# State rows spread by DMA, h in PSUM, sums on PE, and a new order for a batch's chain in a fused Mamba and mixture-of-experts kernel

## Chip, cores and metric

One core of one Trainium2 chip (trn2). The metric is the device time of one execution in microseconds (us).

## What is computed

x is (4, 128, 256): batch, channel, token. Every token is normed over its 128 channels; the channels form 4 chunks of 32 that go through one small Mamba block (inner width 64, 16 states, rank 2):

```python
xz = x @ in_proj.T; xi, z = split(xz)
xc = silu(causal_conv4(xi) + conv_b)
dt, B, C = split(xc @ x_proj.T)
dt = softplus(dt @ dt_proj.T + dt_b)
h = exp(dt * A) * h + (dt * xc) * B[s]        # for each of 16 states s, a scan over tokens
y = (sum_s h * C[s] + xc * D) * silu(z) @ out_proj.T
```

The result plus the scaled input is normed, projected to 128 channels (x1), normed again with the router's norm, and sent through 16 experts of width 256: the two best experts per token get softmax weights, `silu(x Wg) * (x Wu)` is projected back by Wd, weighted and added to x1. All in float32.

## The kernel before

It is written engine by engine with counted semaphores; each engine runs its own list in the order written, SP only issues DMAs. A tile of N = 512 columns holds two chunks of one batch's 256 tokens, its 128 partitions hold 2 x 64 inner channels, so one batch is one tile and the scan has 4 x 16 = 64 steps k (batch k // 16, state k % 16).

One step: ACT writes the decay exp(dt A) into PSUM (`decay`, L434), POOL multiplies dtx = dt xc with the B row of the state (`scan_input`, L286) into u, DVE scans (`scan`, L608) and multiplies h with the C row (`weigh`, L619) into hc. For steps 0 to 31 PE adds hc up in PSUM with an identity matmul (`sum_state`), for steps 32 to 63 POOL adds it to y (`add_state`, L292). B rows go through DRAM: a DMA writes them to B_far and two DMAs per step (L214, each 64 partitions) read one row 64 times into a ring of 4 slots. C rows stay in SBUF, split into two rounded parts (`round_bc`, `bc_rest` L569), and PE spreads them into PSUM with a selection matmul per step (`spread_c`).

The order: a head (loads, norm, projections, convolution, softplus of batch 0), then FIRST = 32 steps with the softplus pieces of batches 1 to 3 at steps 1 to 15 (`factor_1`, `factor_2`, `add_relu`, `scan_source`), then 64 items n = (batch n // 16, expert n % 16), of which the first 32 each have a step (k = 32 + n) beside them. In an item PE does `up` (L853), `down` of two items before (L868), `gate` of the next item (L835), then `spread_c`; ACT does `gate_tanh` (L485) of the next item and a decay; DVE does `gate` (L662), `scan`, `hidden` (L672), then `weigh` of the step before; POOL does u, adds hc, and once per two items multiplies the tokens with a row of gate weights (`scale_tokens`, xs, L316), which an ACT-issued DMA spreads from DRAM (Gs, `spread_gate`).

Between the last step of a batch and its first expert lies a chain of small pieces (`back`): D x and gating (L628, L631), output projection, norm, projection, second norm with the router's logits, top 2, weights, their transposition to rows in DRAM. Two tables, BESIDE_STEPS and BESIDE_ITEMS, say at which of the 16 slots after the batch's last step an engine does which piece; the piece is done at the end of the engine's loop body. `back` on ACT loads the ln and exp table before each reciprocal root and the tanh table after it once the experts run. The first row of gates of the next batch is asked for at item 13 of 16.

The SP list: x, Wg, Wu, rows of batch 0, four steps' B rows, Wd, rows of batch 1, then the rest.

Of the kernel before, what the change touches and what calls it, by code (L numbers as in the profile page):

```python
# [14 lines left out]
P = 128  # L15
# [43 lines left out]
for _name, _width in (("norm_g", 1), ("norm_b", 1), ("proj_b", 1), ("skip", 1), ("conv_w", TAPS), ("conv_b", 1),  # L59
                      ("D", 1), ("dt_b", 1), ("A_log", NS), ("in_x", P), ("in_z", P), ("bc", P), ("dt_in", P),  # L60
                      ("dt_out", P), ("out0", P), ("out1", P), ("proj", P), ("router", E)):
    COLS[_name] = (_at, _at + _width)
    _at += _width
# [3 lines left out]
def build(nc, x, params, gate_w, up_w, down_w, out):  # L67
    with ExitStack() as ctx:
# [20 lines left out]
        def sum_bank(b):  # L89
            return 6 if b < BATCH - 1 else 3  # L90
# [17 lines left out]
        proj_w = sb("proj_w", [P, P])  # L108
        bias = sb("bias", [P, 1])
        shift = sb("shift", [P, 1])  # L110
        iota_e = sb("iota_e", [P, BLK, E])
        unit = sb("unit", [P, 2 * NS])
# [9 lines left out]

        top = sb("top", [P, BLK, 8])
        topi = sb("topi", [P, BLK, 8], U32)
        topf = sb("topf", [P, BLK, 2])
        w01 = sb("w01", [P, BLK, 2])
        e1 = sb("e1", [P, BLK, 1])
        combine = sb("combine", [P, BLK, E])
        CE = sb("CE", [E, BATCH, T])
        Gs = sb("Gs", [P, G_RING, N])  # L130

        xs = sb("xs", [P, 2, N])

# [26 lines left out]
        eps_in, eps, zero, rest_row, quad1, quad2 = (cst[:, i:i + 1] for i in range(6))  # L160
# [771 lines left out]
```

## Time and profile before

| | us |
|---|---|
| median of three runs | 328.30 (328.22 to 331.42) |
| the profiled execution, its own time | 329.45 |
| its span, first to last instruction | 327.6 |
| PE busy, DVE busy, POOL busy, ACT busy | 286.3, 244.3, 179.2, 151.8 |

Times below are from the profiled execution and count from the start of its span. Engines are PE (matmul), DVE (vector), ACT (scalar), POOL (GpSimd), SP (DMA issues). A row of the timeline is start, duration, engine, line, operation, operands; in brackets the idle time before it and the instruction that ended it. Matmuls overlap, and a group's mean mixes instructions in flight: starts, not durations, give PE's rate. Tile names are the profile's: u, h, hc and the B rows are all "ring", th is "dt", hid is "zs" and "y", tn is "xm".

### The profile page before, as it was taken

How to read it: one execution, taken by the hardware profiler on the slowest of the kernel's cores; microseconds unless marked ns; L12 is line 12 of the kernel's file. 1: busy time of each engine (PE TensorE's matmuls, PEld its weight loads, DVE VectorE, ACT ScalarE, POOL GpSimd, SP SyncE). 2: the span in 40 equal slices, each digit the busy share in tenths (PEclk: the TensorE clock that was granted, in tenths of full speed). 3: DMA queues.
4: the chain of work that ended last, by engine and by line, in shares of the span. 5: the costliest groups of instructions: out<-in, count | busy, mean ns of one | idle time of the engine just before them, and what ended most of it. 6: DMA issues, size and time to landing. Idle time of an engine off the chain costs nothing.

```text
span 327.6 us, 3741 instructions
## 1 busy us (share of the span) xinstructions
PE 286.3 (87%) x1120; PEld 199.0 (61%) x1120; DVE 244.3 (75%) x366; ACT 151.8 (46%) x220; POOL 179.2 (55%) x184
## 2 busy tenths in 40 slices
PE   7987397877984798999888899988999999999996
PEld 6734122223431266676566576765688888888885
DVE  2499989999697378898977989797884565555553
ACT  3679546541551334765433365743426363222231
POOL 4001659986357173888799688878861214331310
PEclk9999879996998799999999999999999999999999
DMA  7913975443241330433223423430111111221110
GB/s 261 348 35 107 254 210 168 148 139 127 79 136 57 120 128 33 120 105 96 96 94 125 123 80 114 122 89 19 66 48 44 54 32 34 72 74 58 41 32 18
DMA packets 21621, 33.64 MB, mean 103 GB/s; under 512 B 2848, under 2 KB 8032, under 8 KB 21600
## 3 DMA queue, kind: packets, MB, share of 16 engines
q1 hardware_dynamic: 16720, 24.39, 24.0%
q10 hardware_dynamic: 4880, 9.00, 8.9%
q8 instruction: 9, 0.15, 0.2%
q14 instruction: 12, 0.10, 0.1%
HBM read 32.53 MB, written 0.85 MB: 102 GB/s over the span
## 4 chain that ended last, share of the span: by engine, by line
PE 35%; issue 22%; POOL 15%; DVE 4%; POOLq 0%; DVEq 0%
PE bank L853 10%; PE bank L868 10%; PE bank L835 9%; POOL xs L316 6%; POOL y L292 5%; PE bank L712 4%; POOL ring L286 3%; DVE ring L608 2%; DVE ring L619 2%; POOL chk L304 1%; PE bank L789 0%; PE bank L788 0%; DVE zs L672 0%; POOL w L300 0%; DVE X L676 0%
## 5 line engine op out<-in xcount | busy, mean ns | idle before, releaser
L485 ACT ACTIVATE dt<-bank,cst 128x512 f32<-128x512 f32 x64 | 44.0, 687 | 112.4 <-PE bank L835 112.3
L286 POOL TENSOR_TENSOR ring<-dtx,ring 128x512 f32<-128x512 f32 x64 | 81.0, 1277 | 18.2 <-DVE ring L608 11.4
L608 DVE TENSOR_TENSOR_SCAN ring<-bank,ring 128x512 f32<-128x512 f32 x64 | 77.6, 1213 | 7.1 <-issue 6.7
L853 PE MATMUL bank<-xs,Wu 128*128 128x256 f32 x256 | 68.0, 388 | 10.3 <-POOL xs L316 5.6
L316 POOL TENSOR_TENSOR xs<-xm,Gs 128x512 f32<-128x512 f32 x32 | 41.4, 1294 | 59.1 <-DMA Gs<-CE_far 54.9
L662 DVE SCALAR_TENSOR_TENSOR dt<-dt,bank 128x512 f32<-128x512 f32 x64 | 43.6, 682 | 36.5 <-ACT dt L485 36.5
L835 PE MATMUL bank<-xm,Wg 128*128 128x256 f32 x256 | 65.7, 379 | 0.0
L434 ACT ACTIVATE bank<-dt,cst,A 128x510 f32<-128x510 f32 x64 | 49.7, 777 | 30.4 <-DVE ring L608 28.0
L853 PEld LDWEIGHTS bank<-xs,Wu 128*128 128x128 f32 x256 | 46.3, 190 | 22.6 <-issue 13.0
L835 PEld LDWEIGHTS bank<-xm,Wg 128*128 128x128 f32 x256 | 48.6, 190 | 7.0 <-issue 0.5
L619 DVE TENSOR_TENSOR ring<-ring,bank 128x512 f32<-128x512 f32 x62 | 41.6, 671 | 14.9 <-PE bank L712 14.6
L292 POOL TENSOR_TENSOR y<-y,ring 128x512 f32<-128x512 f32 x30 | 38.2, 1272 | 23.7 <-DVE ring L619 23.5
L712 PE MATMUL bank<-C_rows,sel 64*128 64x512 f32 x64 | 33.7, 528 | 19.2 <-DVE ring L619 13.4
L712 PEld LDWEIGHTS bank<-C_rows,sel 64*128 64x128 f32 x64 | 12.4, 194 | 52.4 <-DVE ring L619 30.8
L712 PE MATMUL bank<-ring,ident 128*128 128x512 f32 x64 | 39.6, 706 | 0.0
L868 PE MATMUL bank<-zs,Wd 128*128 128x256 f32 x128 | 32.9, 380 | 0.2 <-DVE y L628 0.2
L868 PE MATMUL bank<-y,Wd 128*128 128x256 f32 x128 | 32.8, 379 | 0.0
L868 PEld LDWEIGHTS bank<-zs,Wd 128*128 128x128 f32 x128 | 24.2, 190 | 3.8 <-issue 0.5
L868 PEld LDWEIGHTS bank<-y,Wd 128*128 128x128 f32 x128 | 24.3, 190 | 3.3
L672 DVE TENSOR_TENSOR zs<-dt,bank 128x512 f32<-128x512 f32 x32 | 21.6, 675 | 3.5 <-PE bank L712 1.1
L672 DVE TENSOR_TENSOR y<-dt,bank 128x512 f32<-128x512 f32 x32 | 21.5, 673 | 2.5 <-PE bank L853 0.8
L274 POOL TENSOR_TENSOR dtx<-dt,xc 128x512 f32<-128x512 f32 x4 | 5.1, 1286 | 26.3 <-DVE dt L592 26.3
(108 smaller groups left out, 229.7 us busy)
## 6 DMA issues: line engine op xcount, KB each, us to landing
ring<-B_far SPq DMA_DIRECT2D x128, 128.0 KB, 3.0
Gs<-CE_far ACTq DMA_DIRECT2D x32, 256.0 KB, 3.3
Wg<-gate_w SPq DMA_DIRECT2D x1, 2048.0 KB, 10.3
Wu<-up_w SPq DMA_DIRECT2D x1, 2048.0 KB, 15.7
par<-params ACTq DMA_DIRECT2D x1, 533.5 KB, 4.2
X<-x SPq DMA_DIRECT2D x2, 256.0 KB, 4.5
out<-X SPq DMA_DIRECT2D x4, 128.0 KB, 2.2
B_far<-B_rows SPq DMA_DIRECT2D x4, 64.0 KB, 2.6
```

Source lines behind the costliest of these rows:

```text
L286: g.tensor_tensor(u[:, k % 3], dtx[:, k // NS, :], Bs[:, k % B_RING], ALU.mult).then_inc(S["u_r"], 1)
L292: g.tensor_tensor(y[:, k // NS, :], y[:, k // NS, :], hc[:, k % 3], ALU.add).then_inc(S["acc_r"], 1)
L316: g.tensor_tensor(xs[:, pr % 2, :].rearrange("p (e t) -> p e t", t=T), tn[:, b:b + 1, :].broadcast_to([P, 2, T]), Gs[:, pr % G_RING, :].re ...
L434: a.activation(rows[0], rows[1], ACT.Exp, scale=A[:, s:s + 1], bias=zero).then_inc(S["dA_r"], 1)
L485: a.activation(th[n % 2], bank[gate_bank(n)][:], ACT.Tanh, scale=0.5, bias=zero).then_inc(S["th_r"], 1)
L608: v.tensor_tensor_scan(h[:, k % 3], bank[da_bank(k)][:], u[:, k % 3], 0.0, ALU.mult, ALU.add)\
L619: v.tensor_tensor(dst, h[:, k % 3], bank[c_bank(k)][:], ALU.mult).then_inc(S["hc_r"], 1)
L662: v.scalar_tensor_tensor(th[n % 2], th[n % 2], 1.0, bank[gate_bank(n)][:], ALU.add, ALU.mult)\
L712: return t.matmul(o, w, r, start=start, stop=stop).then_inc(S[name], 1)
L835: o = t.matmul(bank[gate_bank(n)][:, f * T:(f + 1) * T], Wg[:, e, f * P:(f + 1) * P], tn[:, b, :], start=True, stop=True)
L853: o = t.matmul(bank[up_bank(n)][:, f * T:(f + 1) * T], Wu[:, e, f * P:(f + 1) * P], xs[:, pr % 2, ts], start=True, stop=True)
L868: o = t.matmul(bank[sum_bank(b)][:, 0:T], Wd[:, e, f, :], hid[n % 4][:, f * T:(f + 1) * T], start=e == 0 and f == 0, stop=e == E - 1 and f ...
```

## The change

B and C rows of a state stand next to each other in DRAM (BC_far), and one DMA per step brings both, 128 partitions x 1024 columns, into a ring of 6. The C splitting, the selection tile and `spread_c` are gone. The scan writes h into PSUM; `weigh` multiplies it with the C row in SBUF, and in the items it follows its own step's `hidden`. u and hc have rings of 4, and u is made two steps ahead. D x is a matmul that opens each batch's sum; for batches 2 and 3 PE also adds the last state and y ("total"). x1 is made off the chain: the router's input comes from `centred_w` (the projection with its mean taken out) plus the centred x, x1 by two matmuls and one ACT piece later. top, weights and their mixing move from POOL to DVE. The pieces have new slots, and on PE `back` comes first in a step and directly after `up` in an item. Two warming matmuls per step are added. The experts begin at step 28, so 36 items have a step beside them. The first row of gates of the next batch is asked for at item 14 of 16. Wd is loaded ahead of all rows. th, hid, L and oh have tiles of their own.

```diff
-FIRST = 2 * NS
+FIRST = 28
 ITEMS = BATCH * E
 BESIDE = STEPS - FIRST
-LAST_C2 = FIRST - 2
 LAG = 2
-B_RING = 4
+BY_PE = 2 * NS
+BC_RING = 6
 G_RING = 3
-
-
-BESIDE_STEPS = {"DVE": {1: 0, 5: 5, 6: 7, 9: 12, 10: 14, 12: 16},
-                "POOL": {12: 16},
-                "PE": {2: 1, 3: 3, 5: 6, 6: 8, 7: 10, 9: 13, 13: 17},
-                "ACT": {3: 2, 4: 4, 7: 9, 8: 11, 10: 15, 13: 18}}
-BESIDE_ITEMS = {"DVE": {1: 0, 4: 5, 5: 7, 8: 12, 9: 14, 11: 16},
-                "POOL": {11: 16},
-                "PE": {2: 1, 3: 3, 5: 6, 6: 8, 7: 10, 9: 13, 12: 17},
-                "ACT": {2: 2, 3: 4, 6: 9, 7: 11, 10: 15, 12: 18}}
-
-F32, F32R, U32 = mybir.dt.float32, mybir.dt.float32r, mybir.dt.uint32
+U_RING = HC_RING = 4
...
+BESIDE_STEPS = {"DVE": {1: "gated", 4: "norm", 6: "tokens", 7: "top", 8: "mix"},
+                "PE": {1: "out", 2: "var", 4: "centre", 5: "var_t", 7: "logits", 8: "turn", 9: "x1"},
+                "ACT": {1: "sq", 2: "rstd", 4: "sq_t", 5: "rstd_t", 7: "exp", 8: "gates", 9: "x1", 10: "spread"}}
+BESIDE_ITEMS = {"DVE": {0: "gated", 3: "norm", 6: "tokens", 7: "top", 8: "mix"},
+                "PE": {0: "total", 1: "out", 2: "var", 4: "centre", 5: "var_t", 7: "logits", 9: "turn", 10: "x1",
+                       11: "skip_D"},
+                "ACT": {1: "sq", 2: "rstd", 4: "sq_t", 5: "rstd_t", 8: "exp", 9: "gates", 10: "x1"}}
...
-        STATE_SUM = (5, 6)
-
-        def c_bank(k):
-            return (2, 3)[k % 2] if k < LAST_C2 else 3
+        STATE_SUM = (5, 6, 6, 6)
 
         def da_bank(k):
             return k % 2 if k < FIRST else 0
 
+        def h_bank(k):
+            return (7, 3)[k % 2] if k < FIRST else 7
...
+            return 3 if b < BATCH - 1 else 7
...
+        def by_pe(k):
+            return k < BY_PE or k % NS == NS - 1
...
+            sp.dma_start(Wd[:], down_w.rearrange("e (f p) h -> p e f h", p=P)).then_inc(S["wd_in"], 16)
+
+            def spread_bc(k):
                 b, s = divmod(k, NS)
                 if s == 0:
                     sp.wait_ge(S[f"far{b}"], 16)
-                if k >= B_RING:
-                    sp.wait_ge(S["u_r"], k - B_RING + 1)
-                for j in range(2):
-                    sp.dma_start(Bs[DI * j:DI * (j + 1), k % B_RING, :],
-                                 B_far[b, NS * j + s:NS * j + s + 1, :].broadcast_to([DI, N]))\
-                        .then_inc(S[f"Bs_in{k % B_RING}"], 16)
+                if k >= BC_RING:
+                    sp.wait_ge(S["hc_r"], k - BC_RING + 1)
+                row = BC_far[b].rearrange("(j s w) n -> j s (w n)", w=2, j=2)[:, s:s + 1]
+                sp.dma_start(BCs[:, k % BC_RING].rearrange("p w n -> p (w n)"), row.broadcast_to([2, DI, 2 * N]))\
+                    .then_inc(S[f"BC_in{k % BC_RING}"], 16)
...
+            for k in range(BC_RING):
+                spread_bc(k)
...
-                if k + 1 < STEPS:
-                    scan_input(k + 1)
+                if k + 2 < STEPS:
+                    scan_input(k + 2)
+                add_state(k - 1)
                 if n % 2 == 0 and n + 2 < ITEMS and (n + 2) % E:
                     scale_tokens(n // 2 + 1)
                 if n % E == E - 1 and n + 1 < ITEMS:
                     scale_tokens(n // 2 + 1)
-                if k <= STEPS:
-                    add_state(k - 1)
-                back(*chain("POOL", k))
...
+                if item == "exp":
+                    for i in range(BLK):
+                        act.wait_ge(S["top_r"], BLK * b + i + 1)
+                        a.activation(e1[:, i, :], top[:, i, 0:1], ACT.Exp, scale=-1.0, bias=top[:, i, 1:2])\
+                            .then_inc(S["ex_r"], 1)
+                    act.wait_ge(S["ex_r"], BLK * (b + 1))
+                    a.activation(e_sum[:], e1[:], ACT.Copy, bias=1.0).then_inc(S["sum_r"], 1)
...
+                if item == "x1":
+                    act.wait_ge(S["x1p_r"], b + 1)
+                    act.wait_ge(S["bias_r"], 1)
+                    a.activation(X[:, b, :], bank[R][:, T:2 * T], ACT.Identity, bias=bias[:]).then_inc(S["x1_r"], 1)
+                if item == "spread":
+                    spread_gate(0)
+                    spread_gate(1)
...
+                back(*chain("ACT", k), True)
+                if n % E == E - 2 and n + 2 < ITEMS:
+                    spread_gate(n // 2 + 1)
...
+            bc_rows(1)
             for d in range(2):
-                bc_rest(d)
-                if d:
-                    bc_rows(d)
-                    dve.wait_ge(S["brow_r"], d + 1)
-                dve.wait_ge(S["bcl_r"], d + 1)
+                dve.wait_ge(S["brow_r"], d + 1)
                 edge = bank[d][:].rearrange("p (q t) -> p q t", t=T)[:, :, 0:1]
                 v.memset(edge, 0.0).then_inc(S["da0"], 1)
-            bc_rows(2)
 
             def scan(k):
+                if k == 1:
...
+                if h_bank(k) == h_bank(k - 1):
+                    dve.wait_ge(S["hc_r"], k)
+                elif k >= 2:
+                    dve.wait_ge(S["hc_r"], k - 1)
+                v.tensor_tensor_scan(bank[h_bank(k)][:], bank[da_bank(k)][:], u[:, k % U_RING], 0.0, ALU.mult, ALU.add)\
                     .then_inc(S["scan_r"], 1)
...
+                old = k - HC_RING
+                if old >= 0 and by_pe(old):
+                    dve.wait_ge(S["red_r"], red_count(old + 1))
+                elif old >= 0 and old % NS:
+                    dve.wait_ge(S["acc_r"], acc_count(old + 1))
+                dst = y[:, k // NS, :] if k >= BY_PE and k % NS == 0 else hc[:, k % HC_RING]
+                v.tensor_tensor(dst, BCs[:, k % BC_RING, 1], bank[h_bank(k)][:], ALU.mult).then_inc(S["hc_r"], 1)
...
+                if item == "gated":
+                    if b < BY_PE // NS:
+                        dve.wait_ge(S["red_r"], NS * (b + 1))
+                    else:
+                        dve.wait_ge(S["tot_r"], b - BY_PE // NS + 1)
+                    v.tensor_tensor(y[:, b, :], zs[:, b, :], bank[STATE_SUM[b]][:], ALU.mult).then_inc(S["y_r"], 1)
...
+                    dve.wait_ge(S["topi_r"], BLK * (b + 1))
+                    v.tensor_copy(topf, topi[:, :, 0:2]).then_inc(S["topf_r"], 1)
+                    dve.wait_ge(S["topf_r"], b + 1)
+                    for j in range(2):
+                        v.tensor_tensor(oh[:, j], iota_e[:], topf[:, :, j:j + 1].broadcast_to([P, BLK, E]),
+                                        ALU.is_equal).then_inc(S["eq_r"], 1)
...
                 hidden(n)
+                if k < STEPS:
+                    weigh(k)
                 if n % E == 1 and n >= E:
                     result(n // E - 1)
-                if FIRST < k <= STEPS:
-                    weigh(k - 1)
                 back(*chain("DVE", k))
...
+            def skip_D(b):
+                if b == 0:
+                    pe.wait_ge(S["D_w_r"], 1)
+                    pe.wait_ge(S["t2_r"], 1)
+                elif b == 1:
+                    pe.wait_ge(S["abs_r"], BATCH)
+                else:
+                    pe.wait_ge(S["y_r"], b)
+                t.matmul(bank[STATE_SUM[b]][:], D_w[:], xc[:, b, :], start=True, stop=False)
 
             def sum_state(k):
                 b, s = divmod(k, NS)
                 if s == 0:
-                    pe.wait_ge(S["t2_r" if b == 0 else "abs_r"], 1 if b == 0 else BATCH)
+                    skip_D(b)
                 pe.wait_ge(S["hc_r"], k + 1)
-                mm(bank[STATE_SUM[b]][:], ident[:], hc[:, k % 3], "red_r", s == 0, s == NS - 1)
-
-            def spread_c(k):
-                if before(c_bank, k):
-                    pe.wait_ge(S["hc_r"], before(c_bank, k))
-                elif k:
-                    pe.wait_ge(S["bcl_r"], BATCH)
-                    pe.wait_ge(S["brow_r"], BATCH)
-                mm(bank[c_bank(k)][:], sel[64:128, k % NS, :], C_rows[64:128, k // NS, :], "pC")
-
-            pe.wait_ge(S["sel_r"], 1)
+                mm(bank[STATE_SUM[b]][:], ident[:], hc[:, k % HC_RING], "red_r", False, k < BY_PE and s == NS - 1)
...
+                if item == "skip_D" and b + 1 < BATCH:
+                    skip_D(b + 1)
+                if item == "total" and b >= BY_PE // NS:
+                    sum_state(NS * (b + 1) - 1)
+                    pe.wait_ge(S["acc_r"], acc_count(NS * (b + 1)))
+                    mm(bank[STATE_SUM[b]][:], ident[:], y[:, b, :], "tot_r", False, True)
...
+                if item == "centre":
                     pe.wait_ge(S["y3_r"], b + 1)
-                    mm(r, proj_w[:], chk[:, b, :], "pj_r")
-                if i == 8:
-                    pe.wait_ge(S["x1_r"], b + 1)
-                    mm(r, M[:], X[:, b, :], "tc_r")
-                if i == 10:
+                    t.matmul(r, centred_w[:], chk[:, b, :], start=True, stop=False)
+                    mm(r, M[:], X[:, b, :], "tc_r", False, True)
...
+                if item == "x1":
+                    pe.wait_ge(S["ceh_r"], b + 1)
+                    t.matmul(r2, proj_w[:], chk[:, b, :], start=True, stop=False)
+                    mm(r2, ident[:], X[:, b, :], "x1p_r", False, True)
...
+                back(*chain("PE", k))
                 if k:
                     sum_state(k - 1)
-                back(*chain("PE", k))
+                if k < FIRST - 2:
+                    keep_warm(2, 2)
...
+                back(*chain("PE", k))
                 if n >= LAG:
                     down(n - LAG)
                 if n + 1 < ITEMS:
                     gate(n + 1)
-                if FIRST < k <= STEPS:
-                    spread_c(k - 1)
-                if n == 0:
-                    sum_state(FIRST - 1)
-                back(*chain("PE", k))
+                if k - 1 < BY_PE:
+                    sum_state(k - 1)
```

## Rows read from the trace of the kernel before

**Rows 1.** The page, part 4: shares of the chain that ended last, by engine.

```profile
PE 35%; issue 22%; POOL 15%; DVE 4%; POOLq 0%; DVEq 0%
```

**Rows 2.** Busy times by window: us, each engine's busy us (instructions), clock, DMA share, GB/s.

```profile
35.00:113.80 78.80, 59.67 (x118) 22.11 (x118) 65.57 (x88) 37.14 (x55) 49.16 (x46) 0.87 0.47 145
...
113.80:234.40 120.60, 108.26 (x441) 79.57 (x442) 102.55 (x153) 60.44 (x88) 96.87 (x89) 1.00 0.31 94
...
234.40:327.60 93.20, 90.56 (x419) 78.42 (x417) 52.55 (x86) 30.57 (x45) 26.09 (x26) 1.00 0.16 46
```

**Rows 3.** Timeline from 33 to 48 us: start, duration, engine, line, operation [idle before].

```profile
33.18 4.95 POOL L286 TENSOR_TENSOR ring<-dtx,ring 128x512 f32<-128x512 f32 x4
...
35.07 1.22 DVE L608 TENSOR_TENSOR_SCAN ring<-bank,ring 128x512 f32<-128x512 f32 x1 [0.32 <-ACT bank L434]
...
44.64 3.72 POOL L286 TENSOR_TENSOR ring<-dtx,ring 128x512 f32<-128x512 f32 x3 [6.51 <-DMA ring<-B_far]
```

**Rows 4.** Timeline, DVE, two steps that nothing disturbs.

```profile
69.54 1.21 DVE L608 TENSOR_TENSOR_SCAN ring<-bank,ring 128x512 f32<-128x512 f32 x1
...
71.25 1.21 DVE L608 TENSOR_TENSOR_SCAN ring<-bank,ring 128x512 f32<-128x512 f32 x1
```

**Rows 5.** Groups by line: operands, count, busy us, mean ns, idle before and its releaser.

```profile
L631 DVE TENSOR_TENSOR y<-y,zs 128x512 f32<-128x512 f32 x4 | 5.7, 1432 | 0.1
...
L452 ACT ACT_TABLE_LOAD x6 | 7.7, 1283 | 0.1
...
L457 ACT ACTIVATE sq<-sq,cst 128x256 f32<-128x256 f32 x8 | 4.1, 508 | 0.3
...
L402 ACT ACTIVATE bank<-dtx,cst 128x512 f32<-128x512 f32 x4 | 2.7, 687 | 1.2 <-DVE sq L574 1.2
...
L853 PE MATMUL bank<-xs,Wu 128*128 128x256 f32 x256 | 68.0, 388 | 10.3 <-POOL xs L316 5.6 <-DVE zs L672 2.4 <-DVE y L672 2.4
```

**Rows 6.** Timeline from 105 to 116 us: the last scan alone, the start of the experts.

```profile
105.12 1.22 DVE L608 TENSOR_TENSOR_SCAN ring<-bank,ring 128x512 f32<-128x512 f32 x1
...
113.85 1.22 DVE L608 TENSOR_TENSOR_SCAN ring<-bank,ring 128x512 f32<-128x512 f32 x1
...
114.92 1.13 PE L853 MATMUL bank<-xs,Wu 128*128 128x256 f32 x4 [2.49 <-POOL xs L316]
```

**Rows 7.** Timeline from 190 to 193 us: one loop of an expert and a step.

```profile
190.15 1.03 PE L835 MATMUL bank<-xm,Wg 128*128 128x256 f32 x4
...
191.21 0.69 ACT L485 ACTIVATE dt<-bank,cst 128x512 f32<-128x512 f32 x1 [2.38 <-PE bank L835]
...
191.80 0.77 ACT L434 ACTIVATE bank<-dt,cst,A 128x510 f32<-128x510 f32 x1
...
192.84 1.21 DVE L608 TENSOR_TENSOR_SCAN ring<-bank,ring 128x512 f32<-128x512 f32 x1
```

**Rows 8.** Timeline from 234 to 248 us: the last scan, then PE in the tail.

```profile
234.43 1.22 DVE L608 TENSOR_TENSOR_SCAN ring<-bank,ring 128x512 f32<-128x512 f32 x1
...
246.00 0.59 PE L712 MATMUL bank<-chk,skip_w 128*128 128x256 f32 x2
...
246.43 1.03 PE L853 MATMUL bank<-xs,Wu 128*128 128x256 f32 x4
...
247.30 1.03 PE L868 MATMUL bank<-y,Wd 128*128 128x256 f32 x4
```

**Rows 9.** DMA: the page's GB/s slices, issues with KB and us to landing, two windows.

```profile
GB/s 261 348 35 107 254 210 168 148 139 127 79 136 57 120 128 33 120 105 96 96 94 125 123 80 114 122 89 19 66 48 44 54 32 34 72 74 58 41 32 18
...
ring<-B_far SPq DMA_DIRECT2D x128, 128.0 KB, 3.0
...
Gs<-CE_far ACTq DMA_DIRECT2D x32, 256.0 KB, 3.3
...
76.60:81.60 5.00, 4.99 (x9) 2.80 (x9) 4.51 (x5) 0.97 (x2) 3.66 (x4) 0.50 0.31 110
...
48.00:56.00 8.00, 6.76 (x14) 2.24 (x15) 8.00 (x11) 4.54 (x8) 8.00 (x8) 1.00 0.53 168
```

More of the change, by code:

```diff
@@ L339, in _ @@
                     scale_tokens(n // 2 + 1)
-                if k <= STEPS:
-                    add_state(k - 1)
-                back(*chain("POOL", k))
         @block.scalar
@@ L511, in _ @@
                     spread_gate(pr)
-                if n % E == E - 3 and n + 3 < ITEMS:
-                    spread_gate((n + 3) // 2)
-                back(*chain("ACT", k), True)
         @block.vector
@@ L637, in back @@
+            def back(item, b):
+                if item == "gated":
[4 more added lines that the diff above has]
+                    v.tensor_tensor(y[:, b, :], zs[:, b, :], bank[STATE_SUM[b]][:], ALU.mult).then_inc(S["y_r"], 1)
+                if item == "norm":
                     dve.wait_ge(S["brstd_r"], b + 1)
                     v.tensor_tensor(chk[:, b, :], bank[R][:, 0:T], sq[:, b, :], ALU.mult).then_inc(S["y3_r"], 1)
-                if i == 7:
-                    dve.wait_ge(S["pj_r"], b + 1)
-                    v.scalar_tensor_tensor(X[:, b, :], bank[R][:, 0:T], bias[:], X[:, b, :], ALU.add, ALU.add)\
-                        .then_inc(S["x1_r"], 1)
@@ L643, in back @@
-                if i == 12:
+                if item == "tokens":
                     dve.wait_ge(S["trstd_r"], b + 1)
-                    v.tensor_tensor(tn[:, b, :], bank[R][:, 0:T], sq[:, b, :], ALU.mult).then_inc(S["tn_r"], 1)
-                if i == 14:
+                    v.scalar_tensor_tensor(tn[:, b, :], bank[R][:, 0:T], bias_c[:], sq[:, b, :], ALU.add, ALU.mult)\
+                        .then_inc(S["tn_r"], 1)
+                if item == "top":
                     dve.wait_ge(S["lg_r"], b + 1)
-                    v.tensor_copy(L[b].rearrange("p i e -> p (i e)"), bank[R][:, 0:BLK * E]).then_inc(S["L_r"], 1)
+                    v.tensor_copy(L[:].rearrange("p i e -> p (i e)"), bank[R][:, 0:BLK * E]).then_inc(S["L_r"], 1)
@@ L649, in back @@
                     dve.wait_ge(S["L_r"], b + 1)
-                    for j in range(BLK):
-                        v.max(top[:, j, :], L[b][:, j, :]).then_inc(S["top_r"], 1)
-                    for j in range(BLK):
-                        dve.wait_ge(S["top_r"], BLK * b + j + 1)
-                        v.max_index(topi[:, j, :], top[:, j, :], L[b][:, j, :]).then_inc(S["topi_r"], 1)
-                    v.tensor_tensor(e1[:], top[:, :, 1:2], top[:, :, 0:1], ALU.subtract).then_inc(S["dif_r"], 1)
@@ L656, in back @@
-                if i == 16:
-                    dve.wait_ge(S["sum_r"], b + 1)
-                    v.reciprocal(w01[:, :, 0:1], w01[:, :, 0:1]).then_inc(S["w0_r"], 1)
+                    for i in range(BLK):
+                        v.max(top[:, i, :], L[:, i, :]).then_inc(S["top_r"], 1)
+                    for i in range(BLK):
+                        dve.wait_ge(S["top_r"], BLK * b + i + 1)
+                        v.max_index(topi[:, i, :], top[:, i, :], L[:, i, :]).then_inc(S["topi_r"], 1)
@@ L810, in back @@
                     o_.then_inc(S["lg_r"], 1)
-                if i == 17:
+                if item == "turn":
                     pe.wait_ge(S["ce_r"], b + 1)
@@ L915 @@
             put(f"out{q}", a["conv_out_proj_w"], DM * (2 * q + j), DI * j)
-        for part in range(2):
-            for i in range(2):
-                rows = a["conv_x_proj_w"].T[:, RANK + NS * i:RANK + NS * (i + 1)]
-                put("bc", rows, DI * j, 64 * i + 32 * part + NS * j)
+        for i in range(2):
+            rows = a["conv_x_proj_w"].T[:, RANK + NS * i:RANK + NS * (i + 1)]
+            for state in range(NS):
+                put("bc", rows[:, state:state + 1], DI * j, 2 * NS * j + 2 * state + i)
     for q in range(CHUNKS):
```

314 lines of the change are left out of this document (130 added, 184 removed).

## The prediction

> **What bounds the kernel now.** I read the chain that ended last first [rows 1]. Only 35% of it lies on PE, 22% is "issue", 15% POOL: no engine bounds alone, the handshakes between them do. The stages show where [rows 2]. From 35 to 113.8 the first 32 scan steps run alone, with DVE busy for 65.6 of 78.8 us and PE's clock granted at 0.87. From 113.8 to 234.4 steps 32 to 63 run beside experts 0 to 31, and no engine is full (PE 108.3, DVE 102.6, POOL 96.9 of 120.6 us). From 234.4 on, 32 experts are alone and PE bounds (90.6 of 93.2 us). So the sum is made by stage: first scan, scan cadence, start of the experts, cadence beside them, tail.
>
> **Stage 1, up to the scan of step 28.** Before, the first scan starts at 35.07, behind DVE's two splittings of C rows and its copies. Four u run from 33.18 to 38.13, 1.24 each [rows 3], so the first is done at 34.4; with the splittings gone u is last, so the scan starts at 34.5 (gain 0.6). Steps 3 to 5 waited for B rows: POOL idle 6.5 us for its transfer, behind the 2 MB of Wd on the same queue [rows 3]. Wd now stands ahead of the rows: the early loads end near 17 us by the GB/s slices of 8.2 us each [rows 9], 2 MB more at their 348 GB/s are 6 us, and the rows of batch 0 are asked for at 25.5, so I cost it at nothing, and if that cover fails it costs up to 2 us. An undisturbed step takes 1.71 us (scan at 69.54, next at 71.25 [rows 4]): 1.13 from the scan's start to DVE's next start and 0.58 for a weighing. PE's C spread leaves PE, and two warming matmuls of 128 columns (0.21 each, half of a 256-column one [rows 8]) take its place: neither was last there at full clock. 27 steps x 1.71 = 46.2. Softplus keeps its six DVE pieces, 6 x 0.6 = 3.6. The chain of batch 0 now lies in steps 17 to 26. DVE's part: gating 0.6 (before D x and then gating at 1.43; D x is a matmul now, and gating reads PSUM as the weighing does at 0.67), norm 0.4, tokens 0.4, top 1.4 (the seven small pieces as before, an estimated 0.8, and three of some 0.2 that were POOL's), mixing 0.9 (five such) [rows 5]: 3.7. Its waits, by walking the order with these durations: 0.2 at gating, 0.7 at tokens (for the rsqrt), 0.7 at top (for the logits): 1.6. Scan 27 is then at 34.5 + 46.2 + 3.6 + 3.7 + 1.6 = 89.6.
> From there to scan 28: 1.2 to the weighing, 0.7 for it, sum 0.9, gate matmuls 1.0, tanh 0.7, gate 0.6: 5.1, so 94.7. The first two rows of gates (Gs) are asked for at step 26 and land 3.3 later [rows 9], xs 1.3 after: the first up is ready 1.5 us after scan 28, hidden but for some 0.3. Before, the step from scan 31 (105.12) to scan 32 (113.85) took 8.7 [rows 6].
>
> **Stage 2, steps 28 to 63 beside experts 0 to 35.** Without a chain the loop is: gate matmuls start, 1.06, tanh starts, 0.59, decay, 0.77 and a handover, scan, 1.13, hidden, 0.66, a handover of 0.15, up, 0.93, down, 0.87, the gate matmuls after next [rows 7, 8]: 6.2 us for two items, 3.1 each. DVE alone needs 2.91 (1.71 for the step, 0.6 each for gate and hidden), POOL 2.5 x 1.24 = 3.1. Before, PE had the C spread after the gate as well, so DVE's weighing was held.
> The first item costs 3.9 and the next three 3.3 (steps 28 to 31 are still summed by PE): 13.8, so scan 32 is at 108.5.
> The chain of batch 1 lies at items 4 to 15. PE does its pieces now between up and down, that is ahead of the gate matmuls that tanh, and so DVE, waits for; before they stood behind them. So PE's pieces count nearly in full. Over 3.1 per item I get, slot by slot: total and gating 1.0, out (three of 0.43 [rows 8]) 0.8, variance 1.1 (PE waits for the square, which ACT does only after tanh and decay), table loads and rsqrt (2 x 1.28 + 1.0 [rows 5], more than ACT has spare) 1.9, centring -0.2, second variance 0.6, second pair of table loads 1.8, top 1.3, exp and mixing 1.3 (mixing waits for tanh, decay and three small ACT pieces), x1 and skip 1.8. That is 11.4. Then the boundary: the first gate row of the next batch is issued at offset 14 of 16, behind a tanh; before at 13. Issue to landing 3.3, xs 1.3, so 4.6, against 2.1 until up 16 is otherwise ready: 2.5. 13.9 in all; before, scans 32 to 63 took 120.6 us [rows 6, 8], 3.89 an item or 62 a batch. 16 x 3.1 + 13.9 = 63.5. Batch 2 has PE's last sum and the sum of y as well (2 x 0.86), 0.8 more: 14.7, over 15 intervals 61.2. Scan 63 is at 108.5 + 63.5 + 61.2 = 233.2; before at 234.43 [rows 8], with four experts fewer done.
>
> **Stage 3.** Before, from scan 63 to the end 93.2 us: 32 items x 2.59 (three groups of matmuls at 0.865 [rows 8]) = 82.9, chain matmuls 3.3, the last C spread 0.8, and 6.2 at both ends. Now 28 x 2.59 = 72.5, the same 6.2, chain matmuls 5.9 (D x by PE and the sums, x1's two and centring's two), and PE's waits: 0.5 and 0.5 for the two squares, 0.6 for y3 and tokens, 1.8 for the mixing (behind exp, behind a tanh), 0.5 for the gates at x1, 3.0 for the gate row of batch 3: 6.9. Sum 91.5.
> Span 233.2 + 91.5 = 324.7. Its own time was 1.85 above the span (329.45 against 327.6) and the median of the runs is 1.15 below that time: 324.7 + 1.85 - 1.15 = 325.4 us. So 19 us are won before the experts and nearly all given back by the slots.
>
> **Unknown costs.** A scan into PSUM is not in the trace. ACT writes 512 elements into PSUM in 0.69 (its square) and into SBUF in 0.69 (its tanh) [rows 5, 7], so I take 0, and bound it by an estimated 0.1 us either way. On some 50 scans that are on the path this is +-5 us. Transfers: 512 KB a step instead of 256. 168 GB/s were moved at a share of 0.53 [rows 9], so 317 GB/s at most: 1.65 us a step, under 1.71 by a hair. A row is asked for when the weighing six steps before is done, 3.5 us after its scan, and u takes 1.3, so it may take 6 x 1.71 - 4.8 = 5.5 us; 3.0 (with 128 KB now [rows 9]) plus 1.3 for the 384 KB more is 4.3. I take no loss; two in flight together would give 6.2 and (6.2 + 4.8)/6 = 1.83 a step, +3.4 us. SP issues one DMA a step instead of two (0.6 us each), so its queue is lighter. PE's clock: once, in a step that idled for DVE's gating, it was granted at half (0.50 from 76.6 to 81.6 [rows 9]); after 2.5 us before 114.92 it was not, the up there ran at full rate [rows 6]. At each of three boundaries a half clock would add up to 3 us; I take none, 9 at most.
>
> **The rivals.** (A) The slots cost less: tanh and the gate row run further ahead than I walk them, so that the boundary waits (2 x 2.5 + 3.0) and the mixing waits go. For it speaks that xs hardly held PE before (5.6 us in all [rows 5]). 325 - 10 = 315 us.
> (B) Supply and clock: the rows' transfers lengthen under load and the scan cadence is 1.83 to 2.0 (+3 to +8), and the clock halves after boundary waits (+9). Against it: a share of 0.5 in the steps. 336 us.
> (C) The other side, far off: the one transfer of a step is not spread over all engines. Its source is now two groups of 64 equal rows, where both DMAs before had 64 equal rows of one. Every transfer of the kernel before has 16 or more rows outermost, so no row speaks against it. If the two groups become the unit of splitting, two engines carry 262 KB each. An engine moved 168/(0.53 x 16) = 19.8 GB/s [rows 9]: 13.2 us a step, 64 x 13.2 = 845, with 27 before and 92 after some 960 us. It decides as soon as a step's transfer takes over 5.5 us. The Trainium skill, "DMA: Bandwidth & Descriptors", section "Why a DMA increments its semaphore by 16 and not by 1", has this rule: the engine count is the largest up to 16 that divides the outermost dimension of both sides, which would be 2 here. No run so far shows a DMA on fewer engines.
>
> **How the numbers follow.** The forecast, 320 to 331 by itself, 0.35; A 0.28; B 0.20; C 0.17. Faster than 325.0 are A and four tenths of the forecast, 0.42; slower than 331.6 B and C, 0.37; within 1% (about what a measurement of this kernel can tell from no change) 0.21. The range 311 to 346 takes A and B with the +-5 of the scan, and leaves out C and a little.
>
> **What would show it.** Right: scan 27 near 90, scan 28 near 95, scan 63 near 233; PE waiting for xs some 2.5 us at each boundary; 4.0 us an item beside the steps. Wrong: POOL's u waiting for DMA in the first stretch (B or C), a transfer above 5.5 us, a PEclk digit below 9 after 120 us, scans of another length than 1.21, items beside the steps under 3.7 (A).

## The result and the profile after

| | before | after |
|---|---|---|
| median of the compared runs, us | 328.52 (328.22 to 331.42) | 799.82 (797.41 to 800.16) |
| profiled execution, its span, us | 329.45, 327.6 | 800.02, 798.2 |

The ratio is 2.43 with a 95% interval of 2.416 to 2.447. (Ratios here and below leave out runs more than 1.5% above the fastest of their kernel; the medians are of all runs.) The forecast was 325.4 with a range to 346, so it was wrong by a factor; the case that came is rival C, to which the prediction gave 0.17 and 960 us.

The page of the changed kernel: busy times, the GB/s row (slices of 20 us), packets, and the row of the queue that the B and C rows use.

```profile
PE 359.4 (45%) x1196; PEld 257.7 (32%) x1196; DVE 239.7 (30%) x377; ACT 151.7 (19%) x226; POOL 165.8 (21%) x147
...
GB/s 306 92 52 58 52 58 57 53 52 52 52 52 52 52 53 74 52 75 52 63 63 64 63 53 73 61 66 57 74 63 64 52 75 52 77 18 40 40 56 25
DMA packets 19828, 50.73 MB, mean 64 GB/s; under 512 B 928, under 2 KB 6112, under 8 KB 19808
...
q1 hardware_dynamic: 14928, 41.42, 13.7%
```

Read the GB/s row first. Before it went up and down with the work [rows 9]; now it lies flat at 52 for most of the span. A flat row at a rate far under what the same queue moved elsewhere (306 in the first slice) reads like a server that is never idle. And that server is small: the packets of SP's queue (q1) took 13.7% of sixteen engines' span, close to 2/16 = 12.5%.

Groups by line, then the longest waits.

```profile
L282 POOL TENSOR_TENSOR u<-dtx,BCs 128x512 f32<-128x512 f32 x64 | 80.9, 1264 | 523.8 <-DMA BCs<-BC_far 496.6 <-issue 27.2
...
L585 DVE TENSOR_TENSOR_SCAN bank<-bank,u 128x512 f32<-128x512 f32 x64 | 78.8, 1231 | 351.2 <-POOL u L282 320.6 <-issue 30.6
```

```profile
POOL u L282 <- DMA BCs<-BC_far: 496.6, 61, 10.5
...
PE bank L840 <- POOL xs L296: 217.0, 20, 23.9
```

POOL's u waited in 61 of 64 steps for its rows. DVE waited for u, and PE for xs, whose multiplication stands behind the waiting u in POOL's list. The busy times of DVE and POOL did not grow (239.7 for 244.3 us, 165.8 for 179.2). PE's grew by 73 us, at a mean granted clock of 0.68 instead of 0.97, but most of it fell inside the waits. So nearly all of the 471 us is waiting. The timeline of three steps shows the period:

```profile
104.59 1.26 POOL L282 TENSOR_TENSOR u<-dtx,BCs 128x512 f32<-128x512 f32 x1 [9.15 <-DMA BCs<-BC_far]
105.94 1.23 DVE L585 TENSOR_TENSOR_SCAN bank<-bank,u 128x512 f32<-128x512 f32 x1 [8.60 <-POOL u L282]
...
116.03 1.23 DVE L585 TENSOR_TENSOR_SCAN bank<-bank,u 128x512 f32<-128x512 f32 x1 [8.28 <-POOL u L282]
```

10.09 us a step. DMA issues, with KB and us to landing:

```profile
BCs<-BC_far SPq DMA_DIRECT2D x64, 512.0 KB
Gs<-CE_far ACTq DMA_DIRECT2D x32, 256.0 KB, 6.1
...
BC_far<-BC_rows SPq DMA_DIRECT2D x4, 128.0 KB, 24.4
```

524,288 B in 10.09 us are 52 GB/s, 26 for each of two engines. Gs, on all sixteen, landed after 6.1 us instead of 3.3 [rows 9]; that fits two of its sixteen parts standing behind the rows, and was not taken apart.

The packets tell the number of engines too. The packets under 512 B can be counted as one small write of each engine that takes part in a DMA: the kernel before has 2848 = 178 x 16 for its 178 DMAs. Here it is 928 = 50 x 16 + 64 x 2: fifty DMAs that are not of BCs (x, weights, parameters, rows, gates, results) with sixteen each, and 64 with two. So the trace agrees with the rule of the Trainium skill that the prediction cited ("DMA: Bandwidth & Descriptors", section "Why a DMA increments its semaphore by 16 and not by 1"), by which two groups outermost give two engines.

### The profile page after: what moved, and what is told of

Same layout as the page of the kernel before. It is cut to its first block, busy times and chain, and to the rows that moved or that the text cites. A ratio compares the mean times of both kernels' runs of the same rounds, so it can differ in the third digit from the quotient of the medians.

```text
span 798.2 us, 3766 instructions
## 1 busy us (share of the span) xinstructions
PE 359.4 (45%) x1196; PEld 257.7 (32%) x1196; DVE 239.7 (30%) x377; ACT 151.7 (19%) x226; POOL 165.8 (21%) x147
## 2 busy tenths in 40 slices
DMA packets 19828, 50.73 MB, mean 64 GB/s; under 512 B 928, under 2 KB 6112, under 8 KB 19808
## 3 DMA queue, kind: packets, MB, share of 16 engines
q1 hardware_dynamic: 14928, 41.42, 13.7%
## 4 chain that ended last, share of the span: by engine, by line
issue 55%; DMA 17%; POOL 11%; PE 10%; SPq 3%; DVE 2%; ACT 1%; POOLq 0%; DVEq 0%; ACTq 0%
DMA BCs<-BC_far 16%; POOL u L282 4%; POOL y L289 4%; PE bank L855 3%; SPq L219 3%; POOL xs L296 2%; PE bank L840 2%; PE bank L822 2%; PE bank L687 2%; DVE y L535 1%; DMA X<-x 1%; PE bank L691 0%; ACT L439 0%; DVE hc L596 0%; POOL dtx L270 0%
## 5 line engine op out<-in xcount | busy, mean ns | idle before, releaser
L282 POOL TENSOR_TENSOR u<-dtx,BCs 128x512 f32<-128x512 f32 x64 | 80.9, 1264 | 523.8 <-DMA BCs<-BC_far 496.6
L585 DVE TENSOR_TENSOR_SCAN bank<-bank,u 128x512 f32<-128x512 f32 x64 | 78.8, 1231 | 351.2 <-POOL u L282 320.6
L687 PE MATMUL bank<-hc,ident 128*128 128x512 f32 x68 | 64.1, 1042 | 174.7 <-DVE hc L596 174.7
L472 ACT ACTIVATE th<-bank,cst 128x512 f32<-128x512 f32 x64 | 44.0, 687 | 377.2 <-PE bank L822 377.2
L855 PE MATMUL bank<-hid,Wd 128*128 128x256 f32 x256 | 78.9, 440 | 0.0
L651 DVE TENSOR_TENSOR hid<-th,bank 128x512 f32<-128x512 f32 x64 | 43.8, 684 | 85.1 <-PE bank L840 82.7
L643 DVE SCALAR_TENSOR_TENSOR th<-th,bank 128x512 f32<-128x512 f32 x64 | 43.9, 686 | 79.4 <-ACT th L472 79.4
L855 PEld LDWEIGHTS bank<-hid,Wd 128*128 128x128 f32 x256 | 57.6, 227 | 13.0 <-issue 3.0
L296 POOL TENSOR_TENSOR xs<-xm,Gs 128x512 f32<-128x512 f32 x32 | 40.6, 1271 | 63.6 <-DMA Gs<-CE_far 59.5
L691 PEld LDWEIGHTS bank<-mean_w 128*128 128x128 f32 x184 | 39.4, 287 | 34.9 <-issue 33.9
L596 DVE TENSOR_TENSOR hc<-BCs,bank 128x512 f32<-128x512 f32 x62 | 41.8, 676 | 0.0
```

The costliest lines, as they stand in the source:

```text
L282: g.tensor_tensor(u[:, k % U_RING], dtx[:, k // NS, :], BCs[:, k % BC_RING, 0], ALU.mult)\
L296: g.tensor_tensor(xs[:, pr % 2, :].rearrange("p (e t) -> p e t", t=T), tn[:, b:b + 1, :].broadcast_to([P, 2, T]), Gs[:, pr % G_RING, :].re ...
L472: a.activation(th[:, n % 2], bank[gate_bank(n)][:], ACT.Tanh, scale=0.5, bias=zero).then_inc(S["th_r"], 1)
L585: v.tensor_tensor_scan(bank[h_bank(k)][:], bank[da_bank(k)][:], u[:, k % U_RING], 0.0, ALU.mult, ALU.add)\
L643: v.scalar_tensor_tensor(th[:, n % 2], th[:, n % 2], 1.0, bank[gate_bank(n)][:], ALU.add, ALU.mult)\
L687: return t.matmul(o, w, r, start=start, stop=stop).then_inc(S[name], 1)
```

## The experiments

Theory: the two groups outermost put the transfer on two engines, and that is all of the loss. Rivals: the bytes (512 KB instead of 256), or the new order. The edits are shown shortened: `...` marks what is left out, and `slot` stands for the place in the ring.

**The same bytes by two DMAs.**

```diff
-row = BC_far[b]...[:, s:s + 1]; sp.dma_start(BCs[slot], row.broadcast_to([2, DI, 2 * N]))
+for j in range(2):
+    row = BC_far[b]...[j, s:s + 1]; sp.dma_start(BCs[DI * j:DI * (j + 1), slot], row.broadcast_to([DI, 2 * N]))
```

> The changed kernel, but a step's rows come by two DMAs of 64 partitions each, 64 equal rows outermost, the same 512 KB in the same 4 KB rows. Theory (only two engines carry the one DMA of a step): 16 engines share the rows, POOL's u no longer waits for them, a DMA's small completion packets are 16 again, and the time is what the rest of the change gives, 325 us by the prediction's sum. Rival 1 (512 KB a step are too much for the queue whatever the engines): a step of 5 to 10 us stays, 500 to 800 us. Rival 2 (slots cost less than walked): 315 us. Rival 3 (cadence and clock): 336 us.

340.85 us (339.68 to 342.01), ratio to before 1.036 (1.030 to 1.042): 459 us gone. Its page:

```profile
GB/s 264 348 262 78 229 242 252 236 238 239 237 206 250 125 203 159 153 167 144 135 175 195 217 132 179 160 126 125 40 40 31 60 32 4 62 78 42 53 31 16
DMA packets 21748, 50.73 MB, mean 149 GB/s; under 512 B 2848, under 2 KB 8032, under 8 KB 21728
...
q1 hardware_dynamic: 16848, 41.43, 46.4%
...
L283 POOL TENSOR_TENSOR u<-dtx,BCs 128x512 f32<-128x512 f32 x64 | 81.3, 1272 | 22.0 <-DMA BCs<-BC_far 20.9
```

The same 50.73 MB; u's wait fell from 496.6 to 20.9 us. 2848 = (50 + 128) x 16 once more.

**Only the grouping, in the kernel before.**

```diff
-for j in range(2): sp.dma_start(Bs[DI * j:DI * (j + 1), slot], B_far[b, NS * j + s]...broadcast_to([DI, N]))
+row = B_far[b]...[:, s:s + 1]; sp.dma_start(Bs[:, slot], row.broadcast_to([2, DI, N]))
```

> The kernel before, with its two B DMAs of a step made one, two groups of 64 equal rows outermost, 2 KB rows. Theory (two engines): each moves 64 rows of 2 KB, at the 26 GB/s per engine that the changed kernel shows 5.05 us a step; 64 steps are 323 us, with 31 before the first scan and 93 after the last some 447 us. Rival (it is the size of the DMA or the 4 KB rows): 256 KB in 2 KB rows were moved in 3 us, so 328 us as before.

489.1 us, ratio 1.488 (1.477 to 1.499).

```profile
GB/s 291 142 33 138 106 50 59 49 50 50 50 50 50 51 50 50 50 88 68 85 70 70 69 52 88 69 77 69 68 70 70 85 23 46 52 26 74 62 48 12
DMA packets 19701, 33.63 MB, mean 69 GB/s; under 512 B 928, under 2 KB 6112, under 8 KB 19680
...
L284 POOL TENSOR_TENSOR ring<-dtx,ring 128x512 f32<-128x512 f32 x64 | 81.0, 1265 | 202.4 <-DMA ring<-B_far 188.1
```

With nothing else of the change the row is flat at 50 and 928 comes again. The 447 expected missed 42. Some 14 of them are the step, 5.27 us where nothing disturbs it instead of 5.05 (with rows of 2 KB an engine moved 24.9 GB/s). The rest lies in the first steps, of which one took 11.8 us, and beside the experts, at 5.7 us a step. There the gate rows, on the same two engines too, landed after 5.5 us instead of 3.3, which fits but was not taken apart.

**Four groups.** The rows were stored twice in DRAM, so that one DMA has four groups of 32 outermost.

```diff
-row.broadcast_to([2, DI, 2 * N])
+row.broadcast_to([4, DI // 2, 2 * N])
```

> The changed kernel, with the rows stored twice in DRAM, so that a step's one DMA has four groups of 32 equal rows outermost. Theory (as many engines as groups): four engines move 32 rows of 4 KB each, 5.05 us a step at 26 GB/s per engine, 323 + 31 + 92 = some 446 us, and 4 small completion packets per DMA. Rival (any DMA that is not one run of equal rows falls back to two engines, or is slow for another reason): 10.1 us a step and 800 us, as the changed kernel.

481.32 us, ratio 1.464 (1.452 to 1.477). Its page:

```profile
GB/s 285 320 74 92 121 119 119 104 105 104 103 101 104 103 131 104 118 114 115 118 130 103 129 103 127 111 120 128 116 105 128 79 48 30 45 45 35 64 45 12
DMA packets 20404, 51.25 MB, mean 106 GB/s; under 512 B 1248, under 2 KB 6432, under 8 KB 20384
...
q1 hardware_dynamic: 15504, 41.95, 23.5%
```

1248 = 62 x 16 + 64 x 4: four engines (twelve DMAs more write the rows). The share is near 4/16 and the flat slices read 101 to 105 GB/s, again 26 an engine; an undisturbed step took 5.04 us, as expected. The 446 us expected missed 35: some of them lie beside the experts, where the scans were 5.8 us apart; they were not taken apart. Two, four and sixteen engines with the same kernel around them give 800, 481 and 341 us. Four groups are one DMA of 4 KB rows and 512 KB as well, so neither the number of DMAs nor the size of a transfer explains the three times: the cause is settled.

**What is left: 341 against the forecast's 325.** The two-transfer version has every part of the change, and can be held against the forecast's own stages:

| us | forecast | measured |
|---|---|---|
| first scan | 34.5 | 37.4 |
| scan 0 to 27 | 55.1 | 64.1 |
| scan 27 to 28 | 5.1 | 5.2 |
| scan 28 to 32 | 13.8 | 18.7 |
| scan 32 to 48 | 63.5 | 63.6 |
| scan 48 to 63 | 61.2 | 60.0 |
| scan 63 to the end | 91.5 | 91.1 |

All of the 15.5 us lie ahead of scan 32. Windows of this version (us, busy of PE, weight loads, DVE, ACT, POOL, clock, DMA share, GB/s):

```profile
44.00:60.00 16.00, 13.19 (x60) 8.12 (x59) 14.40 (x18) 8.01 (x12) 10.94 (x9) 1.00 1.04 247
60.00:100.00 40.00, 30.54 (x121) 19.08 (x122) 34.38 (x54) 18.10 (x30) 27.49 (x23) 0.96 0.98 231
```

The sixteen engines are full at 231 to 247 GB/s, where I had 317 from rows 9. Is that what holds the steps? The next run leaves the C rows out: DVE weighs h with the B row instead, which is not the sum that the kernel should give, at the same cost for DVE.

```diff
-row = ...[j, s:s + 1];  dst = hc <- BCs[:, slot, 1] * h
+row = ...[j, s:s + 1, 0:N];  dst = hc <- BCs[:, slot, 0] * h
```

> The version with two transfers a step, but each brings only the B row (2 KB per partition instead of 4), and DVE weighs h with the B row in place of the C row: h is weighed by B, which is not the reference's sum, at the same cost. 256 KB a step instead of 512. Theory (the first stretch of the two-transfer version is bound by what the sixteen engines move, 524,288 B at some 238 GB/s = 2.2 us a step): scan cadence falls to the forecast's 1.71, scan 27 comes 9 us earlier, at 92 or so after a first scan at 37.4; the Gs rows land in about 3.3 us instead of 3.5 and more; 340.9 - 9 = some 331 us. Rival (the cadence of 2.3 comes from the new order on the engines, such as the warming matmuls or the waits of the chain on its new slots): cadence stays at 2.2 to 2.3 and the time at 340 or so.

334.87 us (331.43 to 337.58), ratio 1.016 (1.006 to 1.025). A step did not come down to 1.71, so supply was only a part: scans 0 to 27 took 60.0 us. The first items changed more: scan 28 to 32 took 12.8 us instead of 18.7. With half the bytes the first gate rows landed after 3.6 to 5.1 us instead of 4.7 to 6.7, and the first up waited 1.07 us instead of 4.17 and ran at full clock:

```profile
101.98 1.13 PE L841 MATMUL bank<-xs,Wu 128*128 128x256 f32 x4 [1.07 <-POOL xs L297]
```

The traced execution, 337.58 us, is the longest of the four. Its excess lies elsewhere: scan 32 to 48 took 68.1 us instead of 63.6, 2.8 of it behind one boundary, where PE ran at half the clock. So the total understates what the bytes cost. DVE's timeline shows what holds the steps:

```profile
60.07 1.23 DVE L586 TENSOR_TENSOR_SCAN bank<-bank,u 128x512 f32<-128x512 f32 x1
61.22 0.67 DVE L597 TENSOR_TENSOR hc<-BCs,bank 128x512 f32<-128x512 f32 x1
62.02 1.23 DVE L586 TENSOR_TENSOR_SCAN bank<-bank,u 128x512 f32<-128x512 f32 x1
```

The scan starts 0.80 after the weighing; before it was 0.58 (1.71 less 1.13 [rows 4]). With h on two banks, the scan of step k waits for the weighing of step k-2, which is the instruction right ahead of it on DVE; before, h had three slots. Test: a third bank.

```diff
-return (7, 3)[k % 2] if k < FIRST else 7
+return (7, 3, 2)[k % 3] if k < FIRST else 7
```

> The version with half the bytes (B rows alone by two transfers a step, h weighed by B in place of C), but h of the steps before the experts goes round three PSUM banks instead of two, and the scan waits for the weighing three steps back; the warming matmuls in the loop are gone, since their bank is the third. In the half-byte version an undisturbed step took 1.94 us, not the forecast's 1.71: the scan started 0.80 after the weighing, before 0.58. Theory: the scan of step k has to wait for the weighing of step k-2, and that is the very instruction ahead of it on DVE, so DVE can't begin the one while the other ends; 0.22 us a step, some 27 steps = 6 us. Then undisturbed steps take 1.72 to 1.75 here, scan 27 is at 91, and the time 329. Rival: it is PSUM itself (a scan into it and a weighing out of it): then the step stays at 1.94 and the time at 335.

326.97 us (325.83 to 334.21), ratio 0.994 (0.990 to 0.998); scans 0 to 27 in 53.8 us, 28 to 32 in 13.6. DVE again, h still in PSUM:

```profile
58.15 1.22 DVE L584 TENSOR_TENSOR_SCAN bank<-bank,u 128x512 f32<-128x512 f32 x1
59.27 0.68 DVE L595 TENSOR_TENSOR hc<-BCs,bank 128x512 f32<-128x512 f32 x1
59.86 1.22 DVE L584 TENSOR_TENSOR_SCAN bank<-bank,u 128x512 f32<-128x512 f32 x1
```

0.59 after, 1.71 a step. So PSUM itself is not the cost. Of the 9.0 us over the forecast in these 27 steps, the C rows' bytes are 4.1 and the wait on DVE's own predecessor 6.3, less 1.3 by which the forecast was too long. The warming matmuls of the loop went with the bank, but they are not what held the step: the next two runs have none and kept 1.94. The division holds for this order, bytes first: no run has three slots and all of the bytes in all of these steps, so what the bytes cost once the wait is gone stays open.

**A mended version.** Half of the C rows by PE (a float32 selection matmul), which frees the transfers:

> The version with two transfers a step, but for the even steps 2 to 26 PE spreads the C row into PSUM with a float32 selection matmul (64 x 128 by 512 columns, as much as a state sum, 0.86 us), their transfers bring the B row only, and the two warming matmuls per step are gone. Mean bytes a step in the first stretch 393 KB, at 238 GB/s 1.65 us. Theory of supply: the first stretch runs at 1.71 to 1.8 a step, scan 27 at 92 to 95, the whole 340.9 - 8 = some 333 us. Rival: PE, with 0.86 for the sum in each step and 0.86 more in every second, or a halved clock without the warming matmuls, takes the cover away, and the cadence stays above 2.0: 338 us or more.

340.59 us, ratio 1.036 (1.027 to 1.044): no gain, as the rival said. Undisturbed steps came down to 1.94, where the own wait holds them, with no warming matmuls in the loop and with h of every second step in SBUF (hs):

```profile
55.14 1.23 DVE L596 TENSOR_TENSOR_SCAN bank<-bank,u 128x512 f32<-128x512 f32 x1
56.28 0.67 DVE L609 TENSOR_TENSOR hc<-bank,hs 128x512 f32<-128x512 f32 x1
57.09 1.22 DVE L596 TENSOR_TENSOR_SCAN hs<-bank,u 128x512 f32<-128x512 f32 x1
```

The scan of step 4 came 5.4 us behind that of step 3, since a weighing waited 2.7 us for the first spread. With more warming and earlier gate rows:

> As the run before it, and three small things: 22 instead of 16 warming matmul instructions at the very start, 24 between the first gate and the first up, and the first two rows of gates asked for at step 25 instead of 26, ahead of x1. In the two-transfer version the first matmuls of the head ran at half the clock (3.75 instead of 1.95 us for the four of the centring) and the first up stood 4.2 us for xs, after which up and gate ran at half the clock (2.07 and 1.91 us). Theory: 2 us less in the head and 3 us less at the first item than in the run before: 328 us or so, no slower than the kernel before. Rival: the clock of the head doesn't follow the number of warming matmuls, and the first item is held by POOL's queue instead; then within 1 us of the run before.

336.43 us, ratio 1.021 (1.011 to 1.031). The head came 1.9 us earlier, as expected. Of the first item's 3 us nothing came: from scan 27 to 32 it took 20.7 us, the run before 20.2. The clock did hold there, but the earlier issue made ACT wait 3.4 us for the gates' write, and decay and tanh stood behind it. Then three slots for h, two C rows of three by PE, experts from step 30 and the gate row one item earlier:

```diff
-FIRST = 28
+FIRST = 30
-if n % E == E - 2 and n + 2 < ITEMS: spread_gate(n // 2 + 1)
+if n % E == E - 3 and n + 3 < ITEMS: spread_gate((n + 3) // 2)
```

> The changed kernel mended in all that the runs showed: two transfers a step; h of the steps ahead of the experts in SBUF with a ring of three; the C rows of two steps in three before the experts spread by PE with a float32 selection matmul (341 KB a step instead of 512, at 238 GB/s 1.43 us); experts begin at step 30, and the first gate row of a batch is asked for at item 13 instead of 14, after a chain that ends two items earlier; 22 warming matmul instructions at the start and 12 ahead of the first up. By the last version, with half of C by PE (336.4): 6 us less for the own wait, 3 boundaries x 2.6 less, 0.7 more for two more steps alone: 323 us, faster than the kernel before (327 to 328). Rival: the boundary waits come back as another wait (tanh, hid) and PE with up to 1.72 us a step bounds the first stretch: 330.

331.57 us, ratio 1.008 (1.004 to 1.012): 8.6 us over what I expected. The boundary part held, and the run with the old start and slot prices it:

> As the mended one, but the experts begin at step 28 and the gate row is asked for at item 14, as in the changed kernel. Theory: three boundary waits of 2.6 us of PE for xs stay, so 7 us slower than the mended one, 330 us. Rival (the boundary costs little): within 2 us of it.

340.39 us, ratio 1.034 (1.026 to 1.041), so 8.8 us for start and boundaries together; the edit changes both. The two traces, 10.1 us apart, divide it: the old start reaches scan 32 3.3 us later but with two experts more done, which are 2 x 2.59 us of PE, so by this estimate it is 1.9 better. The boundaries cost 4.1 (scan 32 to 48), 3.5 (48 to 63) and, in a tail that is 0.8 shorter in spite of two experts fewer, 4.4. PE's waits for xs with the old start (0.5 us in all in the mended one), and the up behind one of them, at half the clock (1.91 us for four matmuls that take 1.03):

```profile
PE bank L863 <- POOL xs L306: 6.9, 3, 2.5
```

```profile
169.94 1.91 PE L863 MATMUL bank<-xs,Wu 128*128 128x256 f32 x4 [2.54 <-POOL xs L306]
```

What the mended version lost ahead of the experts lay on PE, in the steps with a batch's chain, C spreads and sums:

```profile
90.70:98.90 8.20, 7.44 (x10) 2.50 (x11) 7.79 (x15) 1.93 (x3) 3.02 (x3) 0.50 0.44 129
```

The clock was granted at 0.50 there (its 1.2 GHz level). So C rows by PE only in the first 16 steps, and the warming matmuls ahead of PE's wait for the rows instead of behind it:

```diff
-return 2 <= k < FIRST - 1 and k % 3 > 0
+return 2 <= k < NS and k % 3 > 0
-pe.wait_ge(S["brow_a"], 2); keep_warm(16, 2)
+keep_warm(20, 6); pe.wait_ge(S["brow_a"], 2)
```

> The mended version with two edits. PE spreads C rows only for two steps in three of the first 16 and leaves them to the transfers after that: in the mended version PE had both sums, the chain's pieces and spreads in steps 23 to 27, its clock was granted at half there, and the scans of 23 to 27 were 2.4 to 4.8 us apart, where the version with half the bytes had 1.7 to 3.5. And the warming matmuls ahead of the loop stand before PE's wait for the BC rows, not behind it: in the mended version the first spreads ran at half the clock and the weighing of step 2 waited 2.04 for one. Theory: 3 us less at the start, 4 us less in steps 23 to 27: 325 us against 328 to 329 before. Rival: without C by PE from step 16 on the transfers bind (512 KB at 238 GB/s, 2.2 us a step against 2.14 in the half-byte version's chain steps) and the gain of the chain steps is given back: 328 to 330.

Its eight runs lie between 325.06 and 332.61 with a median of 329.03, and before's thirteen had 328.99; the ratio is 0.994 (0.989 to 0.999). That is level with the kernel before, or better by half a per cent, not the 325 expected: scans 0 to 27 took 60.2 us, and scan 28 to 32 took 15.8 of which 5.9 was one step. With experts from step 32:

> As the one above, but the experts begin at step 32, as in the kernel before. Theory: two more steps alone at 1.7 to 2.2 instead of beside an expert, where a step adds some 3.9 - 2.6 = 1.3 us: 1 to 2 us slower. Rival (the slots of a chain need the slack): faster than it.

332.74 us, ratio 1.012 (1.008 to 1.017): by the two ratios some 6 us slower than the one above. The sign is the theory's, the size three times its 1 to 2 us. The traces show where: scan 63 came 1.2 us earlier, but two more experts were left for the tail, which took 99.0 us instead of 93.5.

## Why the prediction was wrong

**The step that failed** is the transfer's cost in "Unknown costs": 512 KB at 317 GB/s, 1.65 us a step, "under 1.71 by a hair". 317 GB/s was read from transfers on sixteen engines, and the sum used it for one that had two, at 52 GB/s and 10.09 us a step. The right number was in rival C, with its decision point of 5.5 us; its price of 13.2 us a step took 19.8 GB/s for an engine, measured were 26 and 10.09 us. That makes 765 with the rival's own ends; the other 35 are mostly a first scan that came 8 us later than that, steps longer than 10.09 beside the experts (20 us in all), and a tail of 97.4 instead of 92. What was wrong was the weight. "No row speaks against it" was true, but no row spoke for sixteen engines either: every row of a DMA was of another shape, with 16 or more rows outermost. The rule cited gave two engines for the shape in the diff, plainly, and I gave it 0.17.

**The other terms**, by the two-transfer version:
- First scan 34.5: 37.4. The gain of 0.6 was swallowed by the head, where the first matmuls of the centring ran at half the clock (3.75 us). The kernel before has the same sixteen warming matmuls and ran them at full (1.95 us), after nearly the same idle time (0.72 against 0.85 us); what tipped it is not shown. 22 warming matmuls brought the first scan to 35.8. That is a clock term I had only at the boundaries.
- Cadence 1.71: measured 1.94 from the two-bank wait, and 2.2 to 2.3 with the bytes. I looked at what a scan into PSUM costs (measured 1.23 against 1.21 us, inside my +-0.1) and not at what its two slots make it wait for.
- Rate: 317 GB/s extrapolated from a share of 0.53; 231 to 247 when full. My own alternative of 1.83 a step was nearer.
- First items: 18.7 instead of 13.8. The first up stood 4.2 us for xs, where I had 0.3, and PE then ran at half the clock. With half the bytes these items took 12.8 and 13.6 us, so this too comes for the most part from the transfers: the gate rows lay beside 512 KB a step.

```profile
109.52 2.07 PE L841 MATMUL bank<-xs,Wu 128*128 128x256 f32 x4 [4.17 <-POOL xs L297]
...
111.39 1.91 PE L823 MATMUL bank<-xm,Wg 128*128 128x256 f32 x4
```

- Slots: the walk was right. 63.6 for 63.5 and 60.0 for 61.2, and not by chance: over 3.1 us the first seven items of batch 1's chain took 1.0, 1.2, 1.2, 1.9, -0.2, 0.6 and 1.9, where I had 1.0, 0.8, 1.1, 1.9, -0.2, 0.6 and 1.8. The boundary wait:

```profile
175.29 1.13 PE L841 MATMUL bank<-xs,Wu 128*128 128x256 f32 x4 [2.64 <-POOL xs L297]
```

2.64 for the 2.5 forecast, at full rate afterwards. Rival A, that these waits vanish, is out.
- Tail: 91.1 for 91.5, in part by luck. Its waits stayed under their terms (boundary 3.0, mixing 1.8, squares 0.5 each), some 4.6 us in all instead of 6.9, so the rest took 1.9 more than I had:

```profile
PE bank L841 <- POOL xs L297: 4.2, 2, 2.2
PE bank L798 <- DVE combine L640: 1.4, 1, 1.4
...
PE bank L688 <- ACT sq L432: 0.3, 1, 0.3
PE bank L688 <- ACT sq L437: 0.3, 1, 0.3
```

(Waits from scan 60 on: the 4.2 is the boundary of batch 2 with 1.96 and that of batch 3 with 2.24.)

So even on sixteen engines the change is 3.6% slower, near the 336 of rival B. B named two of the parts: the transfers (4 in the steps, and most of the 5 of the first items) and the clock, though at the head and the first up and not, in this trace, at the boundaries. The own wait, 6, it did not have.

## What to carry to other kernels

Before two DMAs are merged into one, write down the outermost dimension of both sides as the instruction carries it, and treat a rate measured on another shape as unknown. In a trace, a flat GB/s row, a queue share near k/16 (where that queue is busy for most of the span) and the count of packets under 512 B tell how many engines a DMA had. When a buffer's ring shrinks, look which instruction its wait now names: if it is the one right ahead on the same engine, the two can't overlap any more, at no change in any duration.

## What was not expected of the hardware

- An engine alone is quicker than one of sixteen: with 2 engines a 4 KB row took 158 ns (64 rows in 10.09 us, 26 GB/s), with 4 about the same, with 16 some 275 ns (8 rows in 2.2 us at 238 GB/s, 15 GB/s each). Each of these DMAs reads one to four rows over and over; whether that or the path is the limit was not tried.
- A scan that waits for the weighing right ahead of it on DVE starts 0.21 us later than without the wait (0.80 against 0.59 us after the start of a weighing of 0.67).
- The clock after an idle PE: after 2.49 [rows 6] and 2.64 us for xs the up ran at full rate, after 2.54, 2.78 and 4.17 at half. The length of that wait alone doesn't decide it.
